# Four decoder blocks on one core: in the first attention, row maxima from wide to narrow, their transposition a unit later, value steps in pairs

## The reference, cut to what matters

```
qkv = (h @ qkv_w + qkv_b).reshape(B, T, 3, H, HD)          # B=2, T=1024, H=16, HD=16
attn = jnp.einsum('bhtd,bhsd->bhts', q, k) * scale
attn = jnp.where(causal[None, None], neg, attn)            # causal = triu(ones, 1)
attn = jax.nn.softmax(attn, axis=-1)
sa = jnp.einsum('bhts,bhsd->bhtd', attn, v).transpose(0, 2, 1, 3).reshape(B, T, C)
```

## Time and profile before

| | |
|---|---|
| median of three runs | 2226.89 us |
| the profiled execution's own time | 2227.47 us |
| its span, first to last instruction | 2225.7 us |
| busy over the span: PE / DVE / ACT / POOL | 92% / 51% / 43% / 34% |
| first unit starts, last value step ends | 115.2 us, 377.1 us |
| busy between 115.2 and 341.4 us: PE / DVE / ACT | 210.7 / 156.0 / 142.7 of 226.2 us |

### The profile page before, as it was taken

One profiled execution on the slowest core, in us unless ns is written; L12 is line 12 of the kernel. 1 busy time (PEld: TensorE's weight loads), 2 busy tenths in 40 slices (PEclk: granted clock), 3 DMA queues, 4 the chain that ended last, 5 costly groups with the idle time before them and its releaser, 6 DMA issues. The chain is left out here.

```text
span 2225.7 us, 27002 instructions
## 1 busy us (share of the span) xinstructions
PE 2055.6 (92%) x10558; PEld 1227.9 (55%) x10558; DVE 1132.0 (51%) x2011; ACT 947.8 (43%) x1443; POOL 750.6 (34%) x504
## 2 busy tenths in 40 slices
PE   5989998798988989999999999999999999999997
PEld 3544443586766854444544454445445867666675
DVE  4666662625354456756555555555553243535353
ACT  5356666233334325555355535553555422222221
POOL 1212100203223116666566656665561011212121
PEclk9999999899998979999999999999999999999999
DMA  7723331000000020200000000000000600000000
GB/s 155 138 31 46 45 55 56 27 1 1 1 1 1 1 64 1 67 1 1 1 1 1 1 1 1 1 1 1 1 1 20 166 16 0 10 1 9 0 10 10
DMA packets 48206, 52.76 MB, mean 24 GB/s; under 512 B 14730, under 2 KB 38988, under 8 KB 47668
## 3 DMA queue, kind: packets, MB, share of 16 engines
q1 hardware_dynamic: 48084, 51.11, 11.1%
HBM read 41.24 MB, written 8.80 MB: 22 GB/s over the span
## 5 line engine op out<-in xcount | busy, mean ns | idle before, releaser
L1844 POOL TENSOR_TENSOR total<-total,pr 128x1024 f32<-128x1024 f32 x183 | 444.1, 2427 | 232.5 <-ACT pr L2054 215.7
L2054 ACT ACTIVATE pr<-sc 128x1024 f32<-128x1024 f32 x256 | 259.8, 1022 | 267.0 <-PE sc L1720 262.4
L1865 DVE TENSOR_REDUCE pmax<-ring 128x1 f32<-128x512 f32 x512 | 314.5, 684 | 98.3 <-PE ring L1668 98.3
L1720 PE MATMUL sc<-q_full,k_full 64*128 64x512 f32 x1024 | 294.9, 589 | 0.0
L1738 PE MATMUL o<-pr,v_pair 128*64 128x512 f32 x1024 | 247.7, 605 | 0.0
L1668 PE MATMUL ring<-k_round,q_round 64*128 64x512 f32 x512 | 214.3, 569 | 5.8 <-DVE k_round L1859 2.0
L629 ACT ACTIVATE probs<-s 128x512 f32<-128x512 f32 (+1 forms) x304 | 163.6, 575 | 106.1 <-PE s L342 59.0
L1029 POOL TENSOR_TENSOR c_scores<-c_scores,c_total 128x1024 f32<-128x1024 f32 (+1 forms) x48 | 77.0, 1614 | 312.9 <-DVE c_total L985 312.9
L1668 PEld LDWEIGHTS ring<-k_round,q_round 64*128 64x128 f32 x512 | 78.7, 190 | 137.3 <-DVE pmax L1865 115.3
L463 DVE TENSOR_REDUCE row_max<-s 128x1 f32<-128x640 f32 (+3 forms) x128 | 127.5, 1021 | 51.3 <-PE s L324 51.1
L1720 PEld LDWEIGHTS sc<-q_full,k_full 64*128 64x128 f32 x1024 | 128.9, 191 | 25.8 <-issue 16.8
(11 more groups left out here) (344 smaller groups left out, 3515.2 us busy)
## 6 DMA issues: line engine op xcount, KB each, us to landing
qk_dram<-qk_parts SPq DMA_DIRECT2D x32, 192.0 KB, 2.7
q_stack<-qk_dram SPq DMA_DIRECT2D x48, 128.0 KB
k_stack<-qk_dram SPq DMA_DIRECT2D x48, 128.0 KB
x<-in_x SPq DMA_DIRECT2D x4, 512.0 KB, 7.7
region<-in_L_xattn_mlp_w SPq DMA_DIRECT2D x2, 1024.0 KB, 7.0
region<-in_L_xattn_ff_w SPq DMA_DIRECT2D x1, 2048.0 KB, 19.0
out<-region SPq DMA_DIRECT2D x8, 256.0 KB, 2.2
region<-in_L_xattn_sa_wo SPq DMA_DIRECT2D x1, 1024.0 KB, 8.3
```

Of the source, the lines that this page charges most:

```text
L1720: ins = te.matmul(s2[at % 2][:, j], kf[n % 2][head[j], keys], qf[n % 2][head[j], halves[half]], start=False, stop=True)
L1844: pool.tensor_tensor(out=total[half][:], in0=other[:], in1=probs[at % KEPT][:], op=ALU.add).then_inc(sums, 1)
L1865: dve.tensor_reduce(part_max[:, j, t, half:half + 1], ring[bank_of_max(i)][:], AX.X, ALU.max).then_inc(s1_free, 1)
L2054: act.activation(probs[here % KEPT][:], s2[at % 2][:], ACT.Exp).then_inc(s2_free, 1)
```

## The change

Three edits, all in the order of the first attention. The maxima of a task are listed from t=7 to t=0 instead of from t=0 to t=7. The turn of the maxima stands one unit later than the even spread would have it; every other step of the maxima stays where it was by number, so the same place now holds another width. Value steps i and i+1 (i even) stand together, where i+1 alone stood before: 3 units behind the last unit that feeds i+1.

```
-TOPS = ([(0, (0, 1, 2, 3)), (1, (0, 1, 2, 3))] + [(t, pair) for t in (2, 3) for pair in ((0, 1), (2, 3))]
-        + [(t, (j,)) for t in range(4, TB) for j in range(4)])
+TOPS = ([(t, (j,)) for t in range(TB - 1, 3, -1) for j in range(4)]
+        + [(t, pair) for t in (3, 2) for pair in ((0, 1), (2, 3))] + [(1, (0, 1, 2, 3)), (0, (0, 1, 2, 3))])
...
-        tops_before = lambda u: min(G * N1, N1 + LEAD + u * N1 // N2)
-        values_after = lambda u: [(n, i) for n in range(G) for i in range(N3) if n * N2 + last_unit[i] + LAG == u]
+        spread = lambda u: min(G * N1, N1 + LEAD + u * N1 // N2)
+        tops_before = lambda u: spread(u) if u == 0 or spread(u) % N1 or spread(u) == spread(u - 1) else spread(u) - 1
+
+        values_after = lambda u: [(n, i) for n in range(G) for i in range(N3) if n * N2 + last_unit[i | 1] + LAG == u]
```

## The result

The changed kernel takes 2210.31 us, the median of four runs (2207.96 to 2212.57), against 2226.23 of the kernel before in the same comparison: a ratio of 0.9927, 95% interval 0.9913 to 0.9942. The medians lie 15.9 us apart; 6.9 were forecast. The sign is right and the time lies just inside the range, but the gain is more than twice the forecast: the forecast was wrong in size. Two steps of it failed above all, the loss of 2 us put down for the units alone and the sum of a cycle, 1.34 instead of 2.02.

What follows compares the result with a forecast made beforehand. TensorE was taken to bound the long stretch of the first attention; 8.9 us gained there less 2 lost behind it gives 6.9, so 2220.0 us in the median's measure, range 2210 to 2229.

Steps and rivals of the forecast that it cites:

- the units alone: Behind the last maxima, where ScalarE paces: a pair loses 0.43 us, five wide pairs 2.1; loss taken 2, bounds 0 and 4.
- the sum of a cycle: Long stretch of the first attention: 1.32 + 0.16 + 0.76 - 0.90 = 1.34 us gained per cycle, 8.9 us over 6.64 cycles.
- six pairs: Value steps in the first attention: each pair saves one way into and out of the four strips, 0.22 us; 1.32 a cycle.
- wait for the division: First value step of each half: now 6 units behind the turn of `o` instead of 2, its wait goes, 0.16 us a cycle.
- turn of the maxima: Between two tasks' maxima: a shorter last reduction and two units in between cut the loss from 1.17 to 0.41 us, gain 0.76.
- The rival that halved it: Value step pairs: the second step's first four weight loads stand open, a pair saves 0.11 us, total 2224.3; chance 20%.
- The maxima by width: Maxima steps behind the turn: wide ones in a row make TensorE wait 1.25 us a cycle against 0.35 before, costing 0.90.
- The walk: One cycle followed step by step from the turn of the maxima: waits of 0.33, 0.39, 0.13 and 0.40, 1.25 us in all.
- The slow rival: First attention: two `s1` tensors cannot carry eight wide maxima steps, 3.5 us of waits a cycle, 8 slower: 2235; chance 10%.
- the rival in which VectorE catches up in full: First attention: pairs hide all waits for wide maxima, 6.0 us back, 2 more with the tail's better bound: 2212; chance 18%.

Runs made afterwards that it cites:

- the mixed kernel: The changed kernel with wide and narrow maxima in turn (t=7 with t=4, t=6 with t=5, t=3 with t=2): cycle 32.16 us against 32.07, ratio 0.9942.

## Why the forecast was half of the gain

What is measured against what the sum had, for a cycle:

| term | forecast | measured |
|---|---|---|
| six pairs | -1.32 | -1.39 |
| wait for the division | -0.16 | -0.35 |
| turn of the maxima | -0.76 | -0.75 |
| turn of `o` | 0 | -0.16 |
| waits for maxima | +0.90 | +0.66 |
| sum | -1.34 | -1.99 (cycle: -2.02) |

**Pairs: right.** A block starts 0.093 late, its first pass takes 0.453 where the later ones take 0.429, and from its last pass to the next unit it is 0.545, 0.116 more than a pass. A second step in the block pays none of this again: 0.23 a pair, where I took 0.22. The rival that halved it fell. The trace does not agree with the rule of the Trainium skill ("TensorE: Matmul & The Clock Gate", Part 3, "The mechanism") that a weight load overlaps matmuls in flight only where the row groups differ: the changed kernel's last block, four steps, shows four weight loads at a time while matmuls of the same 128 rows are in flight.

```profile
359.74 0.16 PEld L356 LDWEIGHTS o<-probs,region 128*32 128x32 f32 x8
359.75 2.36 PE L356 MATMUL o<-probs,region 128*32 128x512 f32 x32
360.20 0.13 PEld L356 LDWEIGHTS o<-probs,region 128*32 128x32 f32 x4 [0.30 <-ACT probs L632]
360.63 0.13 PEld L356 LDWEIGHTS o<-probs,region 128*32 128x32 f32 x4 [0.30 <-issue]
```

**The turn of the maxima: right**, 1.27 lost before and 0.52 after; forecast were 1.17 and 0.41.

**The division: a size off.** I took the wait from the earlier trace rows, 1.1 us in six cases. A wait in that view begins when the last columns have run out, about 0.17 us after TensorE could have gone on, and a second wait of 0.11 a cycle was so short that it had no row at all. By starts it is 0.25 and 0.11.

**The maxima by width: the step that failed in its reason.** The walk foretold the waits of the changed kernel fairly, 1.25 against 1.1 lost. Two of its three larger waits are in the trace at 0.39 and 0.40, as said, the one at the third wide step at 0.17 instead of 0.33. The price of 0.90 set against the old kernel was too high: by starts it is 0.66. And I booked the whole rise to the order. The order costs nothing with single steps (0.47 to 0.37); the rise comes only where the pairs are (0.47 to about 0.86 in the old order, 0.37 to 1.1 in the new), and it stays when the widths are mixed.

**The turn of `o`: a term left out.** It gains 0.16 a cycle with the new order, single steps or not, and I had not looked at it. While ScalarE copies `o` out, TensorE has one step of the maxima to compute, and the new order makes that step wider: 128 columns more at one turn (t=5 for t=4; lost 0.415 before, 0.36 now), 256 more at the other (two heads of t=3 for one of t=6; 0.69 and 0.58). In the mixed kernel a step of t=6 stands ahead of the first, and 0.31 are lost.

**Units alone: the largest miss.** From exponential 253 of 304 (counted from 0) to the last value step the kernel before took 35.2 us, the changed one 34.7. I had +2. A pair does cost 0.4 where all eight units have 512 columns: the changed kernel's pair at 349.40 and the next are 5.27 us apart, two single steps over the same units 4.85. In the changed kernel ScalarE stands 1.19 idle once, in the kernel before 0.33 twice.

```profile
349.40 1.92 PE L356 MATMUL o<-probs,region 128*32 128x512 f32 x16
351.26 0.82 PE L342 MATMUL s<-q_stack,k_stack 128*128 128x512 bf16 x3
351.69 1.57 ACT L632 ACTIVATE probs<-s 128x512 f32<-128x512 f32 x3 [1.19 <-PE s L342]
```

But this is one pair of the five I multiplied it by. In the others units of 384 columns and less give ScalarE shorter work, a single step already left it idle, and two waits for the division, nearly half a microsecond each, went. The run with singles in this stretch bears the sign out: 0.8 us longer.

The two misses are 4.7 us in the long stretch (from the first exponential to that of unit 253: 13.6 instead of 8.9) and 2.5 behind it: together the 7.2 us between 6.9 and the attention's 14.1. By the table, times 6.64 cycles, the first is 1.6 from the maxima, 1.3 from the division, 1.1 from the turn of `o` and 0.5 from the pairs, some 4.4 of the 4.7; all four went the same way. The remaining 1.8 us to the measured 15.9 lies in the parts that no edit touches and is within their scatter. The slow rival needed 2.3 us of waits a cycle and had 1.1; the rival in which VectorE catches up in full came nearest in time, 2212, for the wrong reason.

Left open: why about 1.1 us of waits for maxima stay beside the pairs, with the widths in order or mixed. A third `s1` tensor, which would test it, was not run.

## What to carry to other kernels

When matmuls of another array shape are scattered among normal ones, count the ways in and out by start-to-start distances and put such steps together, and try how long a block may be: twos paid, threes gave 0.44 us a cycle back, in waits for VectorE. Order the work ahead of a full stop (here the transposition of all maxima) so that its last piece is the cheapest for the engine that it waits for, and put independent work between that piece and the stop. And test two edits apart before giving one of them the bill: the waits that I put down to the order came only where the pairs were.

## What the runs showed of the hardware

- A block of matmuls on four strips of 32 columns, in among whole-array matmuls, costs 0.093 us going in, 0.024 in its first pass and 0.116 going out (changed kernel, 201.89 to 203.89); inside a block, weights are loaded while matmuls that use the same 128 rows run.
- The views' idle times leave out about 0.17 us in which TensorE's last columns run out (a unit lasts 0.38 and the next starts 0.22 behind it); a wait shorter than that shows only in the distance between starts.
- One kernel, unaltered, took 1844 us in one profile and 1849 in another for the same stretch behind its attention, the difference in three steps of some 1.7 us, with the granted clock lower around each (0.90 against 0.97, 0.96 against 1.00 twice).
